# Two dense layers and a recurrence on one core: TensorE's prologue in another order, the weights Wx loaded last and split by ScalarE and VectorE beside the first nine steps

## What is computed

```
c = layernorm(cond) * gamma + beta                      # 4 x 256
w = gelu(c @ W1 + bias1) @ W2 + bias2                   # 4 x 8192
a1, b1, a2, b2 = split(w, 4), each 4 x 256 x 8          # W2 is 256 x 8192, float32
mid = gelu(x @ base_down + (x @ a2) @ b2.T)
x2  = x + x + mid @ base_up.T + (mid @ b1) @ a1.T
h_t = tanh(x2_t @ Wx + b + h_(t-1) @ Wh)                # 512 steps, h_0 = cond
out = x2 + h
```

## Time and profile before

| | |
|---|---|
| time, median of 3 runs | 527.63 us (527.47 to 527.81) |
| time of the profiled execution | 527.65 us |
| its span, first to last instruction | 525.9 us |
| TensorE busy, VectorE, ScalarE, GpSimd | 505.6, 291.8, 175.2, 22.2 us |
| first tanh of the recurrence starts at | 38.02 us |
| read from HBM | 11.85 MB, the page's best slice at 401 GB/s |

### The profile page before, as it was taken

How to read it: one execution, slowest core, us unless ns; L and a number is a source line. 1 busy time by engine, 2 the same in 40 slices (tenths; PEclk the granted TensorE clock), 3 DMA queues, 4 the chain that set the end, 5 groups by cost and what they waited for, 6 DMA issues and landing times.

```text
span 525.9 us, 33134 instructions
## 1 busy us (share of the span) xinstructions
PE 505.6 (96%) x14756; PEld 471.9 (90%) x14756; DVE 291.8 (55%) x2272; ACT 175.2 (33%) x1158; POOL 22.2 (4%) x35
## 2 busy tenths in 40 slices
PE   9999999999999999999999999999999999998885
PEld 6569999999999999999999999999999999998884
DVE  2535565565556556555655555555655655565553
ACT  3103333333333333333333333333333333333322
POOL 7350000000000000000000000000000000000000
PEclk9999999999999999999999999999999999999999
DMA  8970000000000000000000000000000000000000
GB/s 292 401 213 4 4 14 4 4 14 4 14 5 14 6 7 11 4 14 4 15 4 14 4 6 14 4 14 4 14 4 5 14 4 15 4 14 3 14 6 11
DMA packets 8114, 16.05 MB, mean 31 GB/s; under 512 B 500, under 2 KB 5924, under 8 KB 7972
## 3 DMA queue, kind: packets, MB, share of 16 engines
q1 hardware_dynamic: 7904, 13.90, 7.8%
q10 hardware_dynamic: 68, 0.05, 0.0%
HBM read 11.85 MB, written 2.10 MB: 27 GB/s over the span
## 4 chain that ended last, share of the span: by engine, by line
PE 94%; ACT 3%; issue 1%; DVE 1%; DVEq 0%; POOL 0%; POOLq 0%
PE bank L881 64%; PE bank L801 7%; PE bank L845 4%; PE bank L826 3%; ACT h_ring L462 3%; PE bank L850 2%; PE bank L840 2%; PE bank L821 2%; PE bank L831 2%; PE bank L648 2%; PE bank L682 2%; PE bank L810 1%; PE bank L661 1%; PE bank L785 1%; PE bank L869 1%
## 5 line engine op out<-in xcount | busy, mean ns | idle before, releaser
L881 PE MATMUL bank<-h_ring,whp 128*128 128x52 bf16 x6132 | 243.3, 186 | 13.2 <-ACT h_ring L462 13.2
L544 DVE TENSOR_TENSOR r_ring<-h_ring 128x4 f32<-128x4 f32 x1022 | 136.6, 164 | 205.7 <-ACT h_ring L462 203.2
L462 ACT ACTIVATE h_ring<-bank 128x4 f32<-128x4 f32 x1024 | 142.1, 174 | 320.3 <-PE bank L881 312.5
L881 PE MATMUL bank<-r_ring,whp 128*128 128x52 bf16 x4096 | 220.5, 185 | 0.0
L881 PEld LDWEIGHTS bank<-h_ring,whp 128*128 128x128 bf16 x6132 | 187.9, 96 | 34.2 <-ACT h_ring L462 25.8
L881 PEld LDWEIGHTS bank<-r_ring,whp 128*128 128x128 bf16 x4096 | 174.6, 96 | 0.0
L881 PE MATMUL bank<-l_ring,whp 128*128 128x52 bf16 (+1 forms) x2048 | 157.4, 178 | 0.0
L548 DVE TENSOR_TENSOR l_ring<-r_ring 128x4 bf16<-128x4 f32 x1024 | 136.2, 162 | 0.0
L881 PEld LDWEIGHTS bank<-l_ring,whp 128*128 128x128 bf16 x2048 | 122.5, 96 | 0.0
L801 PE MATMUL bank<-xp,wxp 128*128 128x32 bf16 x1488 | 63.0, 176 | 0.0
L801 PEld LDWEIGHTS bank<-xp,wxp 128*128 128x128 bf16 x1488 | 50.5, 96 | 0.0
(11 more groups left out here) (123 smaller groups left out, 240.4 us busy)
## 6 DMA issues: line engine op xcount, KB each, us to landing
w_sb<-in_L_cond_W SPq DMA_DIRECT2D x16, 512.0 KB, 11.5
out<-o_sb SPq DMA_DIRECT2D x16, 128.0 KB
x_sb<-in_x SPq DMA_DIRECT2D x3, 512.0 KB, 15.2
x_sb<-in_x SPq DMA_DIRECT2D x2, 256.0 KB, 9.6
w_sb<-in_L_cond_W SPq DMA_DIRECT2D x1, 256.0 KB, 3.6
down_sb<-in_L_cond_base_down SPq DMA_DIRECT2D x1, 256.0 KB, 5.0
wh_sb<-in_L_cond_Wh SPq DMA_DIRECT2D x1, 256.0 KB, 11.1
up_sb<-in_L_cond_base_up SPq DMA_DIRECT2D x1, 256.0 KB, 11.3
```

What stands on the lines that cost most here:

```text
L462: nc.scalar.activation(h_ring[:, m, slot(pair, s), 0:B], zt, ACT.Tanh).then_inc(h_ready, 1)
L544: nc.vector.tensor_tensor(r_ring[:, k, q, 0:B], state_before(pair, s, k)[:, 0:B], state_hi_before(pair, s, k)[:, 0:B], ALU.subtract).then_ ...
L881: return nc.tensor.matmul(zbank(p, q, m)[:, col0:col0 + n], whp[part][:, k, P * m:P * (m + 1)], rhs[:, 0:n], start=False, stop=stop, skip_ ...
```

## The change

It does five things.

1. TensorE's list in the prologue is written in another order: the bias products of all four factors come first, the products with A2 next, and x's transposes and the products with `down` behind them; B1's and A1's second halves are cut into quarters with other work between; the numbers and places of the zero matmuls change (72 before, 54 after, of which 16 at the start in both).
2. The loads are issued in another order: W1, A2, x, down, Wh, B2, up, B1, A1, Wx, late x. bias2 is the second small load instead of the last.
3. The first 64 rows of x are loaded in four transfers, one per batch, each to 16 partitions with 4 KB rows (`xa_sb`), and rows 64 to 127 in four transfers of 64 partitions, alternately the lower and the upper half (`xb_sb`).
4. GpSimd no longer splits Wx. In steps 0 to 8 ScalarE casts and VectorE subtracts, in four pieces of 128x128 (`wx_part`, `wx_residue`).
5. One input product and one bias start of step 1 move from step 0 to the end of the prologue.

```
-            sp.dma_start(x_sb[0:T0, :, 0], x[:, 0:T0].rearrange("b p d -> p b d")).then_inc(ld_x[0], 16)
             sp.dma_start(w1_sb[:], W1.rearrange("(k p) n -> p k n", p=P)).then_inc(ld_w1, 16)
+            load_w2(A2)
+            for b in range(B):
+                sp.dma_start(xa_sb[T0 // 4 * b:T0 // 4 * (b + 1)], x[b, 0:T0].rearrange("(q r) d -> q r d", r=4)).then_inc(
+                    ld_xa, 16)
             sp.dma_start(down_sb[:], base_down.rearrange("(k p) n -> p k n", p=P)).then_inc(ld_down, 16)
-            load_w2(A2)
+            sp.dma_start(wh_sb[:], Wh.rearrange("(k p) n -> p k n", p=P)).then_inc(ld_wh, 16)
             load_w2(B2)
...
             load_w2(B1)
+            load_w2(A1)
             sp.dma_start(wx_sb[:], Wx.rearrange("(k p) n -> p k n", p=P)).then_inc(ld_wx, 16)
-            load_w2(A1)
...
-            pool.wait_ge(whp_ready, 1)
-            pool.wait_ge(ld_wx, 16)
-            parts(wx_sb, wxp).then_inc(wxp_ready, 1)
...
+            def wx_part(i, n):
+                if i == 0:
+                    act.wait_ge(ld_wx, 16)
+                    src = wx_piece(wx_sb, n)
+                else:
+                    act.wait_ge(wxr_ready, 2 * n + i)
+                    src = wx_piece(wxres[:, i - 1], n)
+                nc.scalar.copy(wx_piece(wxp[i], n), src).then_inc(wxp_ready[i], 1)
...
+                    if tile == 0 and i in (2, 4, 6, 8):
+                        wx_part(2, i // 2 - 1)
+                    if tile == 0 and i < 8:
+                        wx_part(i % 2, i // 2)
...
+            def wx_residue(i, n):
+                dve.wait_ge(wxp_ready[i], n + 1)
+                if i == 0:
+                    src = wx_piece(wx_sb, n)
+                else:
+                    dve.wait_ge(wxr_ready, 2 * n + 1)
+                    src = wx_piece(wxres[:, 0], n)
+                nc.vector.tensor_tensor(wx_piece(wxres[:, i], n), src, wx_piece(wxp[i], n), ALU.subtract).then_inc(
+                    wxr_ready, 1)
...
+                    if tile == 0 and i < 8:
+                        wx_residue(i % 2, i // 2)
...
+            keep_busy(3, 6)
+            w_half_products(B1, 1, 0)
+            keep_busy(6, 6)
+            w_half_products(B1, 1, 1)
+            keep_busy(8, 6)
             pe.wait_ge(fac_ready[B1], 2)
             turn_factor(B1, b1T_psum)
...
             w_products(A1, 0)
-            keep_busy(6, 7)
+            w_half_products(A1, 1, 0)
+            keep_busy(5, 7)
             pe.wait_ge(v0_ready, 1)
             pe.wait_ge(a1d_ready, 1)
             a1_first_product(0)
-            w_products(A1, 1)
+            w_half_products(A1, 1, 1)
+            bias_start(0, 1, 0)
             pe.wait_ge(ld_wx, 16)
             pe.wait_ge(x2_first, 1)
             for m in range(K2):
                 first_input_product(0, m, 0)
-            bias_start(0, 1, 0)
             first_input_product(1, 0, 0)
-            keep_busy(8, 7)
+            keep_busy(2, 7)
             pe.wait_ge(a1d_ready, 2)
             a1_first_product(1)
-            keep_busy(3, 7)
+            bias_start(0, 1, 1)
+            first_input_product(1, 1, 0)
```

More of the change, by code:

```diff
@@ L144, in adaptive_lowrank_then_recurrence @@
         ld_bias2 = sem("ld_bias2")
-        ld_x = [sem(f"ld_x{n}") for n in range(NTT)]
-        ld_x_more = sem("ld_x_more")
+        ld_xa = sem("ld_xa")
+        ld_xb = sem("ld_xb")
+        ld_x = [sem(f"ld_x{n}") for n in range(1, NTT)]
         ld_down = sem("ld_down")
@@ L197, in adaptive_lowrank_then_recurrence @@
         whp_ready = sem("whp_ready")
-        wxp_ready = sem("wxp_ready")
+        wxp_ready = [sem(f"wxp_ready{i}") for i in range(NPART)]
+        wxr_ready = sem("wxr_ready")
         bp_ready = sem("bp_ready")
@@ L231, in hpre @@
         def hpre(m):
[L232 removed]
+            return bank[7 - m][:, D + B * m:D + B * (m + 1)]
         def slot(pair, s):
@@ L414, in _ @@
                 nc.scalar.activation(gT[:, m, :], hpre(m), ACT.Gelu).then_inc(g_ready, 1)
+            for k in range(K2):
+                act.wait_ge(tr_ready, k + 1)
+                nc.scalar.copy(xT[:, k, :, 0:T0].rearrange("p b (q r) -> p r b q", r=4),
+                               bank[6 + k][:, 0:B * T0].rearrange("p (r b q) -> p r b q", r=4, b=B)).then_inc(tr_moved, 1)
             act.wait_ge(a2T_psum, 1)
@@ L645, in _, with keep_busy @@
             pe.wait_ge(pool_step, 1)
-            def keep_busy(n, spare=0):
+            def keep_busy(n, spare=4, first=False):
                 for _ in range(n):
-                    nc.tensor.matmul(bank[spare][:, D:2 * D], zeros_h[:, 0:P], zeros_h[:, 0:D], start=True, stop=True,
+                    nc.tensor.matmul(bank[spare][:, D:2 * D], zeros_h[:, 0:P], zeros_h[:, 0:D], start=first, stop=first,
                                      skip_group_check=True)
-            keep_busy(WARM)
+            keep_busy(WARM, first=True)
             pe.wait_ge(const_ready, 4)
@@ L709, in a1_first_product @@
                                  stop=True, skip_group_check=True).then_inc(up_psum, 1)
-            pe.wait_ge(ld_x[0], 16)
-            first_transposes(0)
-            first_transposes(1)
-            keep_busy(4)
+            pe.wait_ge(ld_bias2, 16)
+            pe.wait_ge(quadrant_ready, 1)
+            for j in (A2, B2):
+                for c in range(2):
+                    bias_product(j, c)
+            pe.wait_ge(cn_ready, 1)
+            for k in range(K2):
+                last = nc.tensor.transpose(bank[5][:, D + B * k:D + B * (k + 1)], cn[:, P * k:P * (k + 1)],
+                                           ident[0:B, 0:B])
+            last.then_inc(cT_psum, 1)
+            bias_product(B1, 0)
             pe.wait_ge(ld_bias1, 16)
@@ L719, in _ @@
                                  start=True, stop=False, skip_group_check=True)
-            pe.wait_ge(cn_ready, 1)
-            for k in range(K2):
-                last = nc.tensor.transpose(bank[2][:, B * k:B * (k + 1)], cn[:, P * k:P * (k + 1)],
-                                           ident[0:B, 0:B])
-            last.then_inc(cT_psum, 1)
-            keep_busy(4)
-            pe.wait_ge(ld_down, 16)
-            base_down_product(0, 0)
             pe.wait_ge(ld_w1, 16)
@@ L758, in _ @@
             w_products(B2, 1)
+            keep_busy(4)
             pe.wait_ge(ld_up, 16)
@@ L769, in _ @@
                 keep_busy(4, 6)
-            w_products(B1, 0)
-            for c in range(2):
-                bias_product(A1, c)
             pe.wait_ge(upT_ready, 1)
@@ L939, in recurrence @@
                             if tile == 0:
-                                pe.wait_ge(wxp_ready, 1)
+                                for part in range(NPART):
+                                    pe.wait_ge(wxp_ready[part], 4)
                         e = i - FILL
```

104 lines of the change are left out of this document (52 added, 52 removed).

## The result

The changed kernel takes 536.76 us (median of 5 runs, 534.59 to 538.34), the kernel before 527.5 us beside it: a ratio of 1.0174, with a 95% interval of 1.0146 to 1.0202. The sign was forecast, the size was not: 9.3 us instead of 1.55, and the time lies outside the range. The profiled execution took 534.59 us, 6.94 more than that of before; it is the fastest of the five, so it shows the least of what is lost.

A forecast was written before the change was run, and what follows sets the result against it. TensorE's own order was taken to bound the prologue, and one loop from tanh through remainders to last matmuls the steps. Prologue -2.45 plus steps +4.0 gave +1.55 us on 527.65: 529.2 us, range 526.8 to 531.6.

The forecast's parts named there:

- What bounds the kernel: Whole kernel: TensorE's own order sets the prologue, not transfers; closer following of loads wins at most some 3 us.
- Up to A2: Prologue until A2's products: they start at 11.0 instead of 12.93, 1.95 us gained.
- A2 to B1: Prologue from A2's products to B1's end: 15.5 us instead of 15.4, B1 ending at 26.5.
- B1 to the first tanh: Prologue from B1's end at 26.5 to first tanh at 35.6, 2.45 us gained in all.
- Wx beside the steps: Early steps: VectorE's subtraction waits for the same step's cast and delays the next remainders, 3.95 us lost, say 4.0.
- At nothing: Items costed at zero: GpSimd's Wx instructions and memset, late x rows with larger transposes inside the stalls, Wx's landing.
- the fourth: Prologue: clock rises late if bias2 is waited for near 4.9; +2 to +4 us, 531.2; chance 0.08.
- The third rival: Prologue: x arrives late through 16-partition transfers at 43 GB/s; +3 us, 532; chance 0.07.

The follow-up runs named there:

- e5: Kernel before without the twelve zero matmuls behind the cond transposes; four executions: 525.77, 538.38, 538.75 and 538.75 us.
- e13: Kernel of e7 with each bias product replaced by one over 128 rows of zeros, factor biases left out; ratio 0.9993.
- e14: Kernel before with eight float32 zero products, 4 rows and 256 columns, replacing four zero matmuls behind the transposes of x; ratio 1.0169.
- e15: Kernel before with eight float32 zero products, 128 rows and 256 columns, replacing four zero matmuls behind the transposes of x; ratio 1.0046.
- e7: Changed kernel with each Wx subtraction one step later and twelve zero matmuls back behind the cond transposes; ratio 1.0072.
- e9: Kernel of e7 with 24 more zero matmuls between the small products and three more groups before the first tanh; ratio 1.0142.
- e3: Kernel before with only the split of Wx moved to ScalarE and VectorE; ratio 1.0077.
- e4: Changed kernel with each VectorE subtraction of Wx one step later, behind that step's remainders; ratio 1.0093.
- e8: Kernel of e7 with gamma and beta loaded ahead of bias2, hidden layer and A2 first, other bias products spread out as before; ratio 1.0134.
- e1: Changed kernel with twelve zero matmuls put ahead of TensorE's wait for cn; ratio 1.0179, runs from 533.3 to 541.0 us.
- e10: Kernel before with A1 loaded ahead of Wx and A1's third quarter of products ahead of the a1d wait; ratio 1.0001.

## Why the prediction was wrong, step by step

**What bounds the kernel**: right that TensorE's own order and not the loads set the prologue. A1's last piece and Wx had landed by 31.5 in the changed kernel too, and no product waited for a load. The busy share of 96% hides both losses: it was 96% before and is 96% after.

**Up to A2** is the step that failed. It put A2 at 11.0, with the array at the lower of its levels "until about 5.8" and at the upper from there on. A2 started at 14.00. The rise came as early as assumed; what the sum had at nothing is a fall behind it, from about 8.3 to 18.5. Of the 3.0 us, 1.0 is the wait for `cn`: `bias2` was put ahead of `gamma` and `beta` on ScalarE's queue, `beta` landed 4.8 us after its issue, and the prediction had named a wait for bias2 only. The other 2 are small products at 1.2 GHz. The twenty zero matmuls were costed as time that goes; e5 shows that the first twelve of them bear on the first rise, e13 and the pair e14 and e15 that the bias products gathered in their place, over 4 rows, cannot stand in for work over 128. e7 and e9 show that putting zero matmuls back beside them does not help.

**A2 to B1** was 15.5, and took 17.8 (14.00 to 31.25 + 0.57). A2's products at the lower level are 1.7 of that (3.64 against 1.93 in e13), the transposes of x 0.4. At the upper level the step is nearly right: e13 has 15.9.

**B1 to the first tanh**: 9.1 predicted, 9.1 measured (31.82 to 40.96). With its twelve zero matmuls, 2.3 us, added to 35.6, the whole prologue would be 37.9; e13, with the clock up, has 37.8. That this fits to 0.1 is partly luck: e13 reaches A2 0.6 us sooner than such a sum (12.74 against 13.3), its products over 128 rows being shorter, and loses 0.4 of it from A2 to B1.

**Wx beside the steps**: 3.95 predicted, 3.97 measured, 3.96 in e3 (12.54 - 8.58). The first period is as before, the next seven are 0.66, 0.67, 0.47, 0.72, 0.31, 0.66 and 0.47 longer, each within 0.01 of the step's own figures. The chain cast, subtraction, remainders is shown by e3 and e4, and the 0.25 us that step 0 was to save is there too: without the stall its period is 1.46 in e13 and e8 instead of 1.72.

**At nothing**: right in the changed kernel, where the stalls hide it. Without stalls the larger transposes of x and the shorter first period are worth 0.5 us (8.08 in e13 against 8.58).

**The rivals**: the fourth, the clock, was it, with a chance of 0.08. Its size, +2 to +4, was about right for the profiled execution: 2.0 up to A2 and 1.9 behind (17.8 against 15.9). Its form was not. It had a late rise behind a wait, and here the level rose early and fell again among products over 4 rows. 1.55 forecast, the wait 1.0, the clock 3.9 and the 0.4 from A2 to B1 make the 6.9 us of the profiled execution; the other executions lost more, up to 538.34, and were not profiled. The trace of before has no more than four records over 4 rows in a row, so the price of sixteen could not be read there; but the zero matmuls stand in it, and the question to ask was what they are for. The third rival did not happen: x's first rows landed by 12.4 and were wanted at 17.58. The transfer rate fell while they came in, to 228 and 269 GB/s in the windows from 8 to 12 us, and not to 43; by finer windows it was 133 to 193 GB/s from 9 to 11, nearer to 2 us for x than to the 1.2 of the prediction's estimate.

What stays open: how much of the work may be over few rows before the level falls, and what part waits have in it (e8). In before four records of `bias_sb` stand at 11.88 and it holds. The scatter of the changed kernel's runs, 534.6 to 538.3, was not resolved into its causes either; the times of e1 and e5, 533.3 to 541.0 and 525.8 to 538.8, suggest that the first rise comes early or late in one and the same kernel, but only late ones are in their profiles.

## What to carry to other kernels

Before zero matmuls are dropped, or products over few rows gathered in one place, count them twice, as time and as clock: lay out the prologue once at each level, and put the price of the lower one in the sum with its chance. Putting zero matmuls back between such products did not help here. Put helper work for later steps behind what the next step waits for, and never in front of it with a wait for another engine's part of the same step: here the order in VectorE's list cost 4.0 us, the work itself 0.03. A queue of small transfers is a chain too: with `gamma` and `beta` ahead of `bias2` the normalised condition was there 1.0 us sooner (e8).

## What was not expected of the hardware

- TensorE, busy without a gap, fell from 2.4 to 1.2 GHz within sixteen records over 4 rows (e14: they start at 7.70, 0.50 from about 10 to 20 us); through sixteen over 128 rows it stayed (e15: 1.00). The changed kernel has 0.50 from about 8.3 to 18.5 us.
- The granted clock of the profile does not show a late first rise. In e5 it reads 1.00 from 4 to 32 us while sixteen records take 1.94 instead of 1.07; only the lengths of like groups tell it:

```profile
16.00:24.00 8.00, 8.00 (x53) 3.05 (x56) 1.69 (x4) 0.00 (x0) 4.14 (x5) 1.00 1.05 395
```

- A VectorE instruction of 0.29 us lasts 1.1 to 1.2 us when it meets a subtraction of GpSimd, both inputs of it in SBUF (b2d and a1d in e10). A cast of GpSimd does it too: in before the second b2d lasts 0.74 and ends 0.14 behind one, part of the wait ahead of 23.13:

```profile
22.32 0.61 POOL L366 CAST whp<-wres 128x512 bf16<-128x512 f32 x1
...
22.33 0.74 DVE L531 TENSOR_TENSOR b2d<-fac,qmask 128x128 f32<-128x128 f32 x1
```
